# Two-way decay scans of an AdaLN-attention-MoE layer: decays read from PSUM, no scaling of the forward scan, a later numerator bonus, and an earlier x added by GpSimd

## The chip, the cores and the metric

The kernel is one program on one core of a Trainium2 chip. The metric is the device time of one launch in microseconds (us), as the median of several executions. TensorE (PE), VectorE (DVE), ScalarE (ACT), GpSimd (POOL) and the DMA queue that SyncE (SP) issues to run side by side and meet at semaphores.

## The reference

For each of 4 sequences (512 tokens, 512 channels) the layer runs a two-way decaying scan, an RWKV-like mixing block, a second scan, and a routed feed-forward part (32 experts, 8 per token). The part that the change touches, cut short:

```python
def _bi_wkv(r, k, v, w, u, time_emb):
    tf = sigmoid(sum(time_emb))
    decay = exp(-exp(w)) * (0.5 + 0.5 * tf)          # one number per channel and sequence
    ek = exp(min(k, 30)); ekv = ek * v
    nf, df = forward  scans a = a*decay + ekv,  b = b*decay + ek
    nb, db = backward scans of the same
    euk = exp(min(u + k, 30))
    num = nf + nb - ekv + euk * v
    den = df + db - ek + euk
    return sigmoid(r) * num / max(den, 1e-8) * (0.8 + 0.2 * tf)

x1 = bi_wkv(x, side, side, w, u, cond)
h = layernorm(x1); xr, xk, xv = mu*h + (1-mu)*shift(h)
x1 = x1 + (sigmoid(xr Wr) * ek*v/(ek+1e-8)) Wout
h2 = layernorm(x1)                                   # two mixes of it
x = x + x1 + sigmoid(xr2 cWr) * (relu(xk2 cWk)**2 cWv)
x = x + ffn(bi_wkv(x, side, side, w2, u2, cond))
```

## The kernel before

Everything is kept as 128 channels by 512 tokens in fp32, so that one tile is a quarter (K = 4) of a sequence (B = 4). One scan tile is an *item*: a sequence b, a quarter k and a scan w (0 is the first, 1 the second). 32 items pass through a pipeline of *slots*, one item each, spread over three engines:

- DVE, `slot`: `fwd` runs two forward scans (numerator L1312, denominator L1313) into `F` and makes the start values of the backward scans (`ini`, L1315); `clip` caps the keys of the next item (L1302, L1303); one instruction multiplies both forward scans by (1 - decay) times (1 + decay) (L1348), which makes one backward scan of the result equal to forward plus backward minus the doubled term; `fin` of the item before (L1340); `bwd` runs the two backward scans (L1324), adds the bonus `EU` to the denominator (L1328) and floors it (L1330, which signals `den_ready`).
- ACT: `pre` takes the exponentials of the next item's keys (L1079, L1080), `post` makes the inverse of the denominator as exp(-ln) (L1086, L1088).
- POOL: `mid` makes ekv and euk*v of the next item (L1008, L1009), `post` adds the bonus to the numerator (L1015) as soon as the backward scans are done, then multiplies numerator and denominator by the inverse (L1017, L1019). `fin` waits for these.

The decay is a 128x1 column of an SBUF table, read by the scans as a broadcast row.

Around the slots a software pipeline runs over the sequences: a prologue (4 items of sequence 0, layer norm and mixes of it), 4 items of sequence 1 with the first projections, then a loop of two iterations of 8 slots each, and a last iteration of 8 slots. Iteration b does, beside its slots, the gates and projections of sequence b, layer norm 2 and the second mixing of sequence b-1, and layer norm 1 of sequence b+1. `center`, `normalise` and `mixes` are DVE's part of a layer norm, `own` (L1128) is ACT's part of the mixing, `product`, `residual`, `final_a` and `y_stage` are DVE steps that read or feed the matmuls. At an iteration's end `add_mix` on POOL adds the mixing result to x (L1047), `x_new` adds that to the residual stream (L1416), and `x_side` (L1423) forms the tile that is stored.

All order is the order in which each engine's program is written; engines wait on counting semaphores. A layer norm's mean goes to PSUM bank 5, its variance to bank 6. After the loops come the routing, a scatter by POOL, the expert matmuls and the output.

## Time and profile before

| | us |
|---|---|
| median of 3 runs | 1420.02 (1419.4 to 1423.0) |
| the profiled execution | 1419.25 |
| its span in the profile | 1417.5 |
| PE / DVE / ACT / POOL busy in the span | 1124.3 / 835.8 / 452.9 / 707.3 |
| granted TensorE clock, mean | 0.921 |

The span divides into a part with scans (up to about 680 us) and a part without. Busy sums over the whole span mix the two, so the reading goes by stretches.

### The profile page before, as it was taken

Reading aid. Unit: us, or ns where it says so; the run is one execution under the profiler, and the core shown is the slowest. Engines: PE = TensorE matmul, PEld = TensorE weight load, DVE = VectorE, ACT = ScalarE, POOL = GpSimd, SP = SyncE. Lnnn points to the kernel's source line nnn. Section 1 sums busy time; section 2 is a strip of 40 time slices with the busy share of each in tenths; the row PEclk is TensorE's granted clock in tenths of the full one; section 3 lists DMA queues with packets and bytes.
Section 4 is the critical chain, followed back from the end, with each engine's and each line's share of the span. In section 5 each row is a group of like instructions: output and inputs, shape, how many; then the busy total and the mean of one; then the engine's idle time right before and its main releaser. Section 6 shows DMA issues by size and latency. Waiting matters only on the chain.

```text
span 1417.5 us, 14264 instructions
## 1 busy us (share of the span) xinstructions
PE 1124.3 (79%) x3686; PEld 653.7 (46%) x3687; DVE 835.8 (59%) x1409; ACT 452.9 (32%) x692; POOL 707.3 (50%) x493
## 2 busy tenths in 40 slices
PE   0155698558963789637899999999799999999938
PEld 0022243223421334213545444444688888888823
DVE  8777568979788995997607830000344444444424
ACT  2233345243352334431412120210233334333310
POOL 5616305645237442566010276775277777777730
PEclk9978799879987789869999999999899999999969
DMA  4979401001110111021412077226677777777685
GB/s 130 363 261 351 144 0 37 15 31 66 59 37 15 37 60 59 30 89 55 177 59 89 37 243 251 106 108 204 158 127 130 128 126 124 126 129 129 96 203 183
DMA packets 132114, 169.11 MB, mean 119 GB/s; under 512 B 9456, under 2 KB 104688, under 8 KB 132080
## 3 DMA queue, kind: packets, MB, share of 16 engines
q1 hardware_dynamic: 102896, 129.37, 29.5%
q0 software_dynamic: 29184, 39.34, 15.0%
q8 instruction: 15, 0.25, 0.1%
q14 instruction: 19, 0.16, 0.0%
HBM read 84.92 MB, written 83.76 MB: 119 GB/s over the span
## 4 chain that ended last, share of the span: by engine, by line
PE 36%; DVE 20%; POOL 18%; issue 18%; DMA 5%; ACT 3%; SPq 0%; POOLq 0%; DVEq 0%; ACTq 0%
PE banks L520 10%; PE banks L541 10%; POOL slots_in L407 9%; DVE arena L1324 4%; PE banks L1530 4%; PE banks L457 4%; PE banks L510 3%; PE banks L531 2%; POOL arena L1009 2%; DVE arena L1401 2%; POOL arena L1008 2%; DVE arena L1328 2%; POOL arena L1019 2%; DMA slots_in<-arena 2%; POOL arena L1015 2%
## 5 line engine op out<-in xcount | busy, mean ns | idle before, releaser
L1530 PE MATMUL banks<-arena 128*128 128x512 f32 x896 | 420.6, 630 | 162.0 <-ACT arena L1145 67.7
L1530 PEld LDWEIGHTS banks<-arena 128*128 128x128 f32 x896 | 179.8, 203 | 400.9 <-issue 237.3
L420 POOL DMA_INDIRECT sums<-arena x160 | 249.5, 1559 | 119.6 <-ACT arena L646 86.7
L457 PE MATMUL banks<-arena 128*128 128x512 f32 x576 | 252.5, 599 | 10.0 <-ACT arena L620 7.1
L407 POOL DMA_INDIRECT slots_in<-arena x128 | 130.1, 1017 | 103.0 <-issue 43.8
L457 PEld LDWEIGHTS banks<-arena 128*128 128x128 f32 x576 | 109.9, 192 | 149.7 <-issue 135.2
L1008 POOL TENSOR_TENSOR arena<-arena 128x512 f32<-128x512 f32 x32 | 64.2, 2006 | 210.4 <-ACT arena L1080 210.4
L520 PE MATMUL banks<-arena 128*128 x640 | 153.3, 383 | 0.0
L541 PE MATMUL banks<-arena 128*128 x640 | 151.2, 379 | 0.0
L807 DVE SCALAR_TENSOR_TENSOR arena<-arena 128x256 f32<-128x256 f32 x160 | 72.1, 490 | 89.5 <-ACT arena L631 89.5
L520 PEld LDWEIGHTS banks<-arena 128*128 128x128 f32 x640 | 116.5, 192 | 13.3 <-issue 0.4
L541 PEld LDWEIGHTS banks<-arena 128*128 128x128 f32 x640 | 115.4, 190 | 12.4
L790 DVE COPY arena<-banks 128x512 f32<-128x512 f32 x80 | 55.3, 691 | 90.8 <-PE banks L510 90.8
L858 DVE TENSOR_TENSOR arena<-arena,banks 128x512 f32<-128x512 f32 x16 | 11.0, 686 | 159.5 <-PE banks L457 159.5
L1324 DVE TENSOR_TENSOR_SCAN arena<-arena 128x512 f32<-128x512 f32 x64 | 104.4, 1671 | 0.2
L631 ACT ACTIVATE arena<-banks 128x512 f32<-128x512 f32 x80 | 47.8, 597 | 162.8 <-PE banks L520 162.8
L1548 PE MATMUL banks<-arena 128*128 128x512 f32 (+1 forms) x64 | 33.8, 670 | 69.7 <-DVE arena L1367 69.6
L1086 ACT ACTIVATE arena<-arena 128x512 f32<-128x512 f32 x32 | 20.1, 630 | 190.4 <-DVE arena L1330 190.4
L646 ACT ACTIVATE arena<-banks 128x512 f32<-128x512 f32 x80 | 47.8, 597 | 90.7 <-PE banks L541 90.7
L1017 POOL TENSOR_TENSOR arena<-arena 128x512 f32<-128x512 f32 x32 | 51.0, 1595 | 47.8 <-ACT arena L1088 47.8
L1401 DVE SCALAR_TENSOR_TENSOR arena<-arena 128x511 f32<-128x511 f32 x80 | 73.7, 974 | 2.0 <-ACT arena L1128 2.0
L617 ACT ACTIVATE arena<-banks 128x512 f32<-128x512 f32 x32 | 19.1, 597 | 164.3 <-PE banks L457 164.3
(169 smaller groups left out, 1418.2 us busy)
## 6 DMA issues: line engine op xcount, KB each, us to landing
slots_in<-arena SPq DMA_DIRECT2D x8, 2800.0 KB, 17.1
arena<-slots_in SPq DMA_DIRECT2D x80, 280.0 KB, 3.2
sums<-arena SPq DMA_DIRECT2D x4, 2176.0 KB, 20.3
arena<-fT SPq DMA_DIRECT2D x32, 256.0 KB, 2.7
arena<-w2T SPq DMA_DIRECT2D x4, 2048.0 KB, 21.4
arena<-w1T SPq DMA_DIRECT2D x4, 2048.0 KB, 12.1
arena<-sums SPq DMA_DIRECT2D x16, 512.0 KB, 8.8
arena<-xT SPq DMA_DIRECT2D x5, 1024.0 KB, 5.6
```

Of the source, the lines that this page charges most:

```text
L407: pool.indirect_dma_start(rows_in, bass.IndirectOffsetOnAxis(ap=POSU[:, n, j:j + 1], axis=0), XLR[:, n], None).then_inc(S['scattered'], 16)
L420: pool.indirect_dma_start(sums[g % RING], bass.IndirectOffsetOnAxis(ap=DESTU[:, g:g + 1], axis=0), YO[:, i % 4, c], None, compute_op=ALU.add)\
L457: ins = pe.matmul(out, w[:, k, m * P:(m + 1) * P], x[k], start=(k == 0), stop=(k == kt - 1))
L520: ins = pe.matmul(bank(2 + q % 2)[:, c * INTER:(c + 1) * INTER], XTB[:, q % 2, c, k], W1[:, bass.ds(e[c], 1), k].rearrange("p o i -> p (o ...
L541: ins = pe.matmul(bank(6 + q % 2)[:, c * LAT:(c + 1) * LAT], HTB[:, q % 2, c, k], W2[:, bass.ds(e[c], 1), k].rearrange("p o i -> p (o i)") ...
L790: dve.tensor_copy(XTB[:, q % 2].rearrange("p c k s -> p (c k s)"), bank(q % 2)).then_inc(S['xT_copied'], 1)
L807: ins = dve.scalar_tensor_tensor(HB[:, q % 2, c], HB[:, q % 2, c], WS[:, bass.ds(2 * i + c, 1)], HB[:, q % 2, c], ALU.mult, ALU.mult)
L1008: pool.tensor_tensor(EV, EK, KV[:, par], ALU.mult).then_inc(S['ev_ready'], 1)
L1017: pool.tensor_tensor(F[:, par, 1], F[:, par, 1], INV, ALU.mult)
L1324: ins = dve.tensor_tensor_scan(F[:, par, n, ::-1], d, F[:, par, n, ::-1], ini[:, par, n:n + 1], ALU.mult, ALU.add)
L1401: ins = dve.scalar_tensor_tensor(out[:, k, 1:T], H[:, k, 1:T], column(RESTG, name, k), out[:, k, 1:T], ALU.mult, ALU.add)
L1530: ins = pe.matmul(out, w[:, k, m * P:(m + 1) * P], x[:, k], start=(k == 0), stop=(k == kt - 1))
```

## The change

What it does:

- The decay table is copied once to PSUM bank 6 (`DECAY`), and all four scans of an item read their decay column from there. Mean and variance of a layer norm now share bank 5 (`STAT`).
- The multiplication by (1 - decay)(1 + decay) (`rest`) is gone from `slot`. The scans stay unscaled; the ratio num/den needs the factor only against the bonus, so the factor is folded into ACT's columns (`less_log`, `log_rest`, `rest`), into the floor (`floors`) and into the start values (`over_rest`). These columns are made once, in the prologue, by a short chain between DVE and ACT.
- POOL's numerator bonus waits for `den_ready` instead of `bwd_done`.
- `add_mix` is replaced by `add_x`: POOL adds x to the residual stream of sequence b-1 at the start of slots 3 to 6 of iteration b, and DVE's `x_new` adds the mixing result directly. The load of x is issued at the head of the iteration instead of near its end.
- `normalise` has one small instruction fewer, and its large one is split in two halves; ACT's `own` starts after the first half.

```diff
+        DECAY = psum[:, 6, 0:2 * K * B].rearrange("p (w k b) -> p w k b", w=2, k=K)
+        STAT = psum[:, 5, :]
@@ SP, iteration
+                    if prev and n == 0:
+                        load_x_again(b - 1)
...
                 elif prev:
-                    load_x_again(b - 1)
                     load_final(b - 1, 0)
@@ POOL
             def post(it):
-                pool.wait_ge(S['bwd_done'], i + 1)
+                pool.wait_ge(S['den_ready'], i + 1)
...
+                    if adds and 3 <= n < 3 + K:
+                        add_x(b - 1, n - 3)
...
-            def add_mix(b):
-                pool.wait_ge(S['xf_loaded'], 16 * (b + 1))
-                for m in range(K):
-                    pool.wait_ge(S['v2_evac'], 4 * b + m + 1)
-                    pool.tensor_tensor(XF[:, m], XF[:, m], R2S[:, m], ALU.add).then_inc(S['x_summed'], 1)
+            def add_x(b, m):
+                if m == 0:
+                    pool.wait_ge(S['z2_ready'], b + 1)
+                    pool.wait_ge(S['xf_loaded'], 16 * (b + 1))
+                whole = XN[:, bass.ds(b, 1), m].rearrange("p o t -> p (o t)")
+                pool.tensor_tensor(whole, whole, XF[:, m], ALU.add).then_inc(S['x_summed'], 1)
@@ ACT
-                act.activation(EU[:, par], EU[:, par], ACT.Exp).then_inc(S['keys_exp'], 1)
+                act.activation(EU[:, par], EU[:, par], ACT.Exp, bias=dcol_of(less_log, it)).then_inc(S['keys_exp'], 1)
...
-                step.did(act.activation(INV, F[:, par, 1], ACT.Ln))
+                step.did(act.activation(INV, F[:, par, 1], ACT.Ln, scale=dcol_of(rest, it)))
                 step.wait()
-                act.activation(INV, INV, ACT.Exp, scale=-1.0).then_inc(S['inv_ready'], 1)
+                act.activation(INV, INV, ACT.Exp, scale=-1.0, bias=dcol_of(log_rest, it)).then_inc(S['inv_ready'], 1)
@@ DVE
-                d = dcol(it).to_broadcast([P, T])
+                d = dcol_of(DECAY, it).to_broadcast([P, T])
                 dve.tensor_tensor_scan(F[:, par, 0], d, EV, 0.0, ALU.mult, ALU.add)
...
-                dve.tensor_scalar(F[:, par, 1], F[:, par, 1], DEN_FLOOR, None, ALU.max).then_inc(S['den_ready'], 1)
+                dve.tensor_scalar(F[:, par, 1], F[:, par, 1], dcol_of(floors, it), None, ALU.max)\
+                   .then_inc(S['den_ready'], 1)
...
-                step.did(dve.tensor_scalar(F[:, it['par']], F[:, it['par']], rest[:, it['w'], it['k'], bass.ds(it['b'], 1)],
-                                           None, ALU.mult))
...
-                step.did(dve.tensor_scalar(TMP, TMP, -0.5, 1.5, ALU.mult, ALU.add))
+                step.did(dve.scalar_tensor_tensor(RS, TMP, 3.0, RS, ALU.subtract, ALU.mult))
                 step.wait()
-                step.did(dve.tensor_tensor(RS, RS, TMP, ALU.mult))
-                step.wait()
-                rs = RS.rearrange("p (o t) -> p o t", o=1).to_broadcast([P, K, T])
-                dve.tensor_tensor(H[:, :, 1:T + 1], H[:, :, 1:T + 1], rs, ALU.mult)\
-                   .then_inc(S[f'norm{which}_ready'], 1)
+                half = K // 2
+                rs = RS.rearrange("p (o t) -> p o t", o=1).to_broadcast([P, half, T])
+                for k in range(0, K, half):
+                    dve.tensor_tensor(H[:, k:k + half, 1:T + 1], H[:, k:k + half, 1:T + 1], rs, ALU.mult)\
+                       .then_inc(S[f'norm{which}_ready'], 1)
...
                 dve.wait_ge(S['x_summed'], 4 * b + m + 1)
-                dve.tensor_tensor(xn(b, m), xn(b, m), XF[:, m], ALU.add).then_inc(S['xnew_ready'], 1)
+                dve.wait_ge(S['v2_evac'], 4 * b + m + 1)
+                dve.tensor_tensor(xn(b, m), xn(b, m), R2S[:, m], ALU.add).then_inc(S['xnew_ready'], 1)
```

How this moves instructions, first on DVE, for one slot of the first four items (`arena` is all of SBUF, `banks` is PSUM; a scan is listed as SCALAR_TENSOR_TENSOR). Before:

```order
L1312 SCALAR_TENSOR_TENSOR arena<-arena 128x512
L1313 SCALAR_TENSOR_TENSOR arena<-arena 128x512
L1315 TENSOR_SCALAR arena<-arena 128x2
L1302 TENSOR_SCALAR arena<-arena 128x512
L1303 TENSOR_SCALAR arena<-arena 128x512
L1348 TENSOR_SCALAR arena<-arena 128x1024
L1340 SCALAR_TENSOR_TENSOR arena<-arena 128x512
L1324 SCALAR_TENSOR_TENSOR arena<-arena 128x512 x2
L1328 TENSOR_TENSOR arena<-arena 128x512
L1330 TENSOR_SCALAR arena<-arena 128x512
```

The same slot on DVE in the changed kernel:

```order
L1339 SCALAR_TENSOR_TENSOR arena<-banks,arena 128x512
L1340 SCALAR_TENSOR_TENSOR arena<-banks,arena 128x512
L1342 TENSOR_SCALAR arena<-arena 128x2
L1329 TENSOR_SCALAR arena<-arena 128x512
L1330 TENSOR_SCALAR arena<-arena 128x512
L1367 SCALAR_TENSOR_TENSOR arena<-arena 128x512
L1350 SCALAR_TENSOR_TENSOR arena<-banks,arena 128x512 x2
L1354 TENSOR_TENSOR arena<-arena 128x512
L1356 TENSOR_SCALAR arena<-arena 128x512
```

The four scans have a PSUM input where they had an SBUF one, the 128x1024 multiplication is gone, and nothing else changes place.

On POOL, the end of a loop iteration before: the last slot's five products and sums, then the four additions of `add_mix`:

```order
L1008 TENSOR_TENSOR arena<-arena 128x512
L1009 TENSOR_TENSOR arena<-arena 128x512
L1015 TENSOR_TENSOR arena<-arena 128x512
L1017 TENSOR_TENSOR arena<-arena 128x512
L1019 TENSOR_TENSOR arena<-arena 128x512
L1044 REGISTER_ALU
L1046 ISA
L1047 TENSOR_TENSOR arena<-arena 128x512
L1046 REGISTER_ALU
L1047 TENSOR_TENSOR arena<-arena 128x512
```

In the changed kernel the additions stand between `post` of one slot (L1023, L1025, L1027) and `mid` of the next (L1016, L1017), here at the start of slot 3:

```order
L1023 TENSOR_TENSOR arena<-arena 128x512
L1025 TENSOR_TENSOR arena<-arena 128x512
L1027 TENSOR_TENSOR arena<-arena 128x512
L1056 REGISTER_ALU
L1058 ISA
L1058 TENSOR_TENSOR arena<-arena 128x512
L1013 REGISTER_ALU
L1016 TENSOR_TENSOR arena<-arena 128x512
L1017 TENSOR_TENSOR arena<-arena 128x512
```

One addition each went from behind the last slot to the head of slots 3, 4, 5 and 6.

On SP's queue the load of x (L906, 128x4x512) now stands at the loop's head between two loads of keys (L889):

```order
L889 ISA [waits euv_ready]
L889 DMA arena<-fT 128x512
L906 ISA
L906 DMA arena<-xT 128x4x512
L887 REGISTER_ALU
L889 ISA [waits euv_ready]
L889 DMA arena<-fT 128x512
```

It stood behind the last store of `q_scratch`, ahead of the two loads of `q_scratch`.

## Rows read from the trace of the kernel before

**Rows 1.** Stretches: length, then busy us (count) of PE, PEld, DVE, ACT, POOL; clock, DMA.

```profile
373.90:543.30 169.40, 121.18 (x256) 52.02 (x255) 144.01 (x151) 65.41 (x92) 81.91 (x48) 0.84 0.13 43
543.30:680.10 136.80, 95.73 (x209) 41.32 (x209) 120.30 (x121) 48.60 (x68) 76.25 (x45) 0.85 0.19 62
```

**Rows 2.** Timeline of DVE over one full slot: start, duration, instruction.

```profile
262.30 1.21 DVE L1312 TENSOR_TENSOR_SCAN arena<-arena 128x512 f32<-128x512 f32 x1
...
264.66 1.05 DVE L1315 TENSOR_SCALAR arena<-arena 128x2 f32<-128x2 f32 x1
...
265.96 1.49 DVE L1303 TENSOR_SCALAR arena<-arena 128x512 f32<-128x512 f32 x1
267.37 0.74 DVE L1348 TENSOR_SCALAR arena<-arena 128x1024 f32<-128x1024 f32 x1
268.03 0.68 DVE L1340 SCALAR_TENSOR_TENSOR arena<-arena 128x512 f32 x1
268.63 3.41 DVE L1324 TENSOR_TENSOR_SCAN arena<-arena 128x512 f32<-128x512 f32 x2
272.08 1.57 DVE L1328 TENSOR_TENSOR arena<-arena 128x512 f32<-128x512 f32 x1
273.68 1.37 DVE L1330 TENSOR_SCALAR arena<-arena 128x512 f32<-128x512 f32 x1
274.97 1.21 DVE L1312 TENSOR_TENSOR_SCAN arena<-arena 128x512 f32<-128x512 f32 x1
```

**Rows 3.** Timeline of POOL over the same slot.

```profile
263.78 1.91 POOL L1017 TENSOR_TENSOR arena<-arena 128x512 f32<-128x512 f32 x1 [1.69 <-ACT arena L1088]
265.65 1.52 POOL L1019 TENSOR_TENSOR arena<-arena 128x512 f32<-128x512 f32 x1
268.71 2.25 POOL L1008 TENSOR_TENSOR arena<-arena 128x512 f32<-128x512 f32 x1 [1.54 <-ACT arena L1080]
270.93 2.17 POOL L1009 TENSOR_TENSOR arena<-arena 128x512 f32<-128x512 f32 x1
273.06 1.71 POOL L1015 TENSOR_TENSOR arena<-arena 128x512 f32<-128x512 f32 x1
```

**Rows 4.** DVE and POOL at the start of a `normalise`, from both timelines.

```profile
338.45 0.75 DVE L1383 SCALAR_TENSOR_TENSOR arena<-banks,arena 128x512 f32<-128x512 f32 x1 [2.60 <-ACT arena L1118]
339.24 1.06 DVE L1385 TENSOR_TENSOR arena<-arena 128x512 f32<-128x512 f32 x1
...
338.49 1.27 POOL L1019 TENSOR_TENSOR arena<-arena 128x512 f32<-128x512 f32 x1
```

**Rows 5.** Stretches of single slots and of the mixes, columns as in rows 1.

```profile
398.85:408.97 10.12, 0.26 (x1) 0.00 (x0) 10.02 (x13) 6.79 (x10) 3.13 (x3) 0.77 0.30 104
420.66:431.50 10.84, 10.84 (x27) 4.84 (x26) 10.74 (x12) 1.15 (x2) 6.06 (x3) 1.00 0.04 5
467.37:477.79 10.42, 6.12 (x15) 2.42 (x13) 10.28 (x12) 3.73 (x5) 5.58 (x3) 0.91 0.00 0
479.98:492.28 12.30, 10.98 (x20) 4.83 (x21) 12.20 (x12) 4.19 (x5) 8.78 (x5) 0.75 0.14 43
515.92:530.06 14.14, 14.14 (x29) 6.06 (x28) 14.14 (x20) 5.70 (x9) 6.19 (x4) 0.84 0.29 107
589.42:625.60 36.18, 17.33 (x41) 7.41 (x39) 35.87 (x34) 5.97 (x10) 24.93 (x13) 0.77 0.23 78
625.60:661.52 35.92, 29.98 (x64) 12.77 (x64) 35.56 (x32) 14.78 (x22) 22.78 (x13) 0.90 0.11 39
```

**Rows 6.** Timeline of DVE: four mixes without and with POOL beside them.

```profile
515.92 2.72 DVE L1401 SCALAR_TENSOR_TENSOR arena<-arena 128x511 f32<-128x511 f32 x4
519.23 4.75 DVE L1401 SCALAR_TENSOR_TENSOR arena<-arena 128x511 f32<-128x511 f32 x4
```

**Rows 7.** Timeline of ACT: an activation with a column operand, and one without.

```profile
392.56 0.69 ACT L1116 ACTIVATE arena<-banks,arena 128x512 f32<-128x512 f32 x1
393.27 0.63 ACT L1118 ACTIVATE arena<-arena 128x512 f32<-128x512 f32 x1
```

More of the change, by code:

```diff
@@ L111, in build @@
         vec = place(len(VECTORS), K)
-        small = place(64)
+        small = place(40)
         tf = small[:, 0:4]
@@ L120, in build @@
         condT = small[:, 32:36]
-        decay = place(2, K, B)
         rest = place(2, K, B)
-        scratch32 = place(2, K, B)
+        over_rest, floors, log_rest, less_log = (place(2, K, B) for _ in range(4))
         ini = place(2, 2)
         MIXES = ['mu_r', 'mu_k', 'mu_v', 'cm_mu_r', 'cm_mu_k']
-        MUG, RESTG, FIRSTB = (place(len(MIXES), K) for _ in range(3))
+        mix_columns = place(3, len(MIXES), K)
+        MUG, RESTG, FIRSTB = (mix_columns[:, n] for n in range(3))
         XN = place(B, K, T)
@@ L143, in build @@
         RS, TMP = (place(T) for _ in range(2))
+        decay, scratch32 = (TMP[:, n * 32:n * 32 + 2 * K * B].rearrange("p (w k b) -> p w k b", w=2, k=K) for n in range(2))
         def q2_again(b, m):
@@ L1055, in _ @@
             with pool.Fori(1, B - 1) as b:
-                slots(body_items(b), body_items(b + 1)[0], b, USUAL)
-                add_mix(b - 1)
-            slots(last_items, None, B - 1, USUAL)
-            add_mix(B - 2)
-            add_mix(B - 1)
+                slots(body_items(b), body_items(b + 1)[0], b, USUAL, True)
+            slots(last_items, None, B - 1, USUAL, True)
+            for m in range(K):
+                add_x(B - 1, m)
             part3_pool(pool)
@@ L1115, in rsqrt @@
                     act.wait_ge(S['xs_ready'], 4 * b)
[L1116 removed]
+                step.did(act.activation(RS, STAT, ACT.Ln, bias=eps_col))
                 step.wait()
@@ L1122, in own @@
             def own(which, b):
-                act.wait_ge(S[f'norm{which}_ready'], b + 1)
                 for n, (name, out) in enumerate(zip(*mixed(which))):
@@ L1127, in own @@
                     for k in range(K):
+                        if n == 0 and k % 2 == 0:
+                            act.wait_ge(S[f'norm{which}_ready'], 2 * b + k // 2 + 1)
                         act.activation(out[:, k], H[:, k, 1:T + 1], ACT.Identity, scale=column(MUG, name, k),
@@ L1210, in _ @@
             ln_exp()
+            act.wait_ge(S['rest_ready'], 1)
+            step.did(act.activation(log_rest, rest, ACT.Ln))
+            step.wait()
+            act.activation(less_log, log_rest, ACT.Exp, scale=-1.0).then_inc(S['log_exp'], 1)
+            act.wait_ge(S['columns_ready'], 1)
             pre(first_items[0])
@@ L1285, in _ @@
             step.did(dve.tensor_tensor(rest, rest, scratch32, ALU.mult))
+            dve.tensor_copy(DECAY, decay)
             step.wait()
-            def dcol(it):
-                return decay[:, it['w'], it['k'], bass.ds(it['b'], 1)]
+            dve.tensor_scalar(rest, rest, 1e-12, None, ALU.max).then_inc(S['rest_ready'], 1)
+            dve.wait_ge(S['rest_ready'], 1)
+            step.did(dve.reciprocal(scratch32, rest))
+            step.wait()
+            step.did(dve.tensor_tensor(over_rest, decay, scratch32, ALU.mult))
+            step.did(dve.tensor_scalar(floors, scratch32, DEN_FLOOR, None, ALU.mult))
+            dve.wait_ge(S['log_exp'], 1)
+            step.wait()
+            step.did(dve.tensor_tensor(scratch32, less_log, rest, ALU.mult))
+            step.wait()
+            step.did(dve.scalar_tensor_tensor(log_rest, scratch32, -1.0, log_rest, ALU.add, ALU.add))
+            step.wait()
+            dve.tensor_scalar(less_log, log_rest, -1.0, None, ALU.mult).then_inc(S['columns_ready'], 1)
             def xn(b, m):
@@ L1507, in _ @@
             residual(0, 3)
-            base, one = step.n, 8 * 3 + 2 * 4
+            base, one = step.n, 8 * 2 + 2 * 3
             with dve.Fori(1, B - 1) as b:
@@ L1547, in mean @@
                         pe.wait_ge(S['y_tile' if which == 1 else 'o_evac'], 4 * b + k + 1)
-                    ins = pe.matmul(bank(5), ones, src[:, k], start=(k == 0), stop=(k == K - 1))
+                    ins = pe.matmul(STAT, ones, src[:, k], start=(k == 0), stop=(k == K - 1))
                 ins.then_inc(S[f'mean{which}_done'], 1)
@@ L1554, in var @@
                 for k in range(K):
-                    ins = pe.matmul(bank(6), ones, src[:, k], start=(k == 0), stop=(k == K - 1))
+                    ins = pe.matmul(STAT, ones, src[:, k], start=(k == 0), stop=(k == K - 1))
                 ins.then_inc(S[f'var{which}_done'], 1)
```

22 lines of the change are left out of this document (11 added, 11 removed).

## The prediction, made before the changed kernel ran

> **What bounds the kernel now.** I read the busy times by stretch first. In a loop iteration of 169.4 us DVE is busy for 144.0 and PE for 121.2; in the last iteration DVE for 120.3 of 136.8, PE for 95.7 [rows 1]. So DVE sets the pace where there are scans, PE has some 48 us of idle time per iteration, and whatever shortens DVE's chain ahead of about 680 us moves all that follows.
>
> Then the timelines of DVE and POOL over one slot, which give what DVE is busy *with*. A slot lasts 12.67 us (262.30 to 274.97). A forward scan alone takes 1.21 us, but the two backward scans take 3.41 where 2 x 1.13 is expected; the addition takes 1.57 and the floor 1.37, the 128x2 product 1.05 [rows 2]. POOL in the same time needs 2.25, 2.17 and 1.71 for products that take 1.27 when it is alone [rows 3, 4]. Set side by side they take turns: POOL's first product is issued at 268.71 while the first backward scan runs (to about 269.77), then runs to 270.93; the second scan runs to about 272.07, and then POOL's second product, to 273.10; DVE's addition ends 0.55 later; POOL's addition follows, to 274.77; DVE's floor ends 0.28 after that. Each of these instructions excludes the other engine's. Some 4.5 of the 12.67 us are DVE waiting inside its own instructions.
>
> **What frees them.** Whether a PSUM operand takes an instruction out of this exclusion is shown at the start of a `normalise`: L1383, with its first input in PSUM and its second in SBUF, runs 338.45 to 339.20 in 0.75 us, and POOL's product beside it takes 1.27, undelayed. The next DVE instruction, with both inputs in SBUF, takes 1.06: it ends 0.55 after POOL's product [rows 4]. The changed scans have just that operand form. The Trainium skill says the same (SBUF — State Buffer, "Who interferes with whom": a Vector instruction with at most one SBUF input, outside the two-port modes, doesn't contend with GpSimd). The trace agrees.
>
> **A slot after the change.** I redo the turn-taking from the durations above, with 0 at the first forward scan.
>
> - *Full slot* (POOL still busy with the item before). POOL's bonus addition runs 0.1 to 1.4 beside the scans, which is free: ACT's ln and exp fill the same 1.5 us. The two products by the inverse run from 1.6 to 2.9 and, with the caps between them, to 4.35 (as 263.78 to 267.17 now). ACT's instructions with a column operand cost 0.06 more each (0.69 against 0.63) [rows 7]; that is in these numbers, twice in the inverse and once in the keys. DVE's scans end at 2.3, the start value waits to 2.9, the caps end at 4.55, the scaling (0.66) is gone, `fin` runs to 5.1. The backward scans, free now, end at 7.4. POOL's products for the next item run from 5.9 (1.26 after the caps, as now, and 0.06) to 8.4. DVE's addition waits for the second, ends at 8.95, and the floor, no longer behind POOL's addition, at 9.4. The next slot starts at 9.3: 3.35 less than 12.67.
> - *With `add_x` in it* (slots 3 and 4): the addition goes in front of `fin` and holds it for 1.2, but DVE loses most of that where it waited for POOL anyway: 9.5, so 3.15 less. `fin` behind slot 4 has no such cover: add_x is issued right as the last product ends and holds it 1.1; with the column operands 1.25 dearer.
> - *POOL idle at its start* (slot 2, 10.84 [rows 5]): 8.0, 2.85 less. Without `fin` (slot 5, 10.42; slot 0 is alike): 7.9, 2.5 less. Slot 6 (12.30), whose forward scans are held now too: 8.65, 3.65 less, `add_x` included. Slot 1 (10.12) is held by ACT's eight `own` in front of the exponentials; these start 1.1 earlier with the split `normalise`: 1.05 less.
>
> **A loop iteration.** Slots 0 to 7: 2.5 + 1.05 + 2.85 + 3.15 + 3.15 + 2.5 + 3.65 + 3.35 = 22.2. The mixes of layer norm 1 lose POOL's `add_mix`: four of them take 4.75 with it beside them and 2.72 without [rows 6], the stretch of 14.14 comes to about 10.6 [rows 5]: 3.5. The two normalises: one small instruction less (0.4 each, like a cap or a floor let in at once), 0.2 each for the split and for ACT's columns: 0.4. Against that the mixes of layer norm 2 get POOL's later addition beside them: -0.6, and `fin` behind slot 4: -1.25. Sum 24.3 of 169.4, twice: 48.6. The row of loads and stores at the iteration's end keeps its length. PE's work of 121 fits into 145; following its order, the mean that opens the next iteration is ready some 2.5 us before DVE wants it.
>
> **The rest.** Last iteration: slots 2 to 4 take 36.18 now and 8.0 + 9.5 + 9.5 = 27.0 after, slots 5 to 7 take 35.92 and 29.5 (ACT is late there with two matmul results, so slot 6 has to wait for its ekv), slot 0 gives 2.5 [rows 5]; less 0.9, since PE's row of 48 matmuls is then the last to finish: 17.4 with the normalise. Prologue: the four first slots give 3.5 + 3 x 3.35 and the layer norm 1.3, the new columns cost 2.2, an estimate (nine tiny instructions in a chain at 0.25; a floor of 512 elements takes 0.28 once it is let in): 12.7. (The very first slot gives 3.5 rather than 2.5, as its first forward scan is held by POOL now.) Second group of four: 2.5 + 2.85 + 3.35 + 2.85, less 0.4 for handoffs, and 0.6 of its layer norm, since PE sets the end there: 11.7. Tail, behind 680 us: 1.2. The load of x moves to a place where 16 DMA engines are 13% busy [rows 1], ahead of a key load that isn't wanted for 20 us: nothing; if it delayed that load, the caps of slot 1 would wait up to 3.
>
> **The unknown price** is that of a scan that reads PSUM. No row has one. Below: nothing, as the scan's own rate (1.13 for 512 elements, against 0.6 for `fin`) is what it waits for. Above: L1383's 0.75 against `fin`'s 0.68 [rows 2, 4], 0.07 for each of 128 scans, 9 us. I take 1.6 in all, near the lower end, as half of the scans lie under POOL's products. The Trainium skill gives VectorE a fixed 120 cycles for a PSUM source and 58 for SBUF (VectorE: DVE Perf Modes, "The TRN2 errata"). By that 65 ns a scan, an estimate, the gain would be 8 us less. The row beside it shows 0.07 at most, so it can't be excluded.
>
> Sum: 48.6 + 17.4 + 12.7 + 11.7 + 1.2 - 1.6 = 90. The profiled execution took 1419.25, so 1329; it lies 0.8 under the median of 1420.02.
>
> **Rivals.**
> 1. *PE takes over* (0.14). DVE's chain gets shorter and PE, at a clock of 0.84 in that stretch, doesn't come along: its 121 us of 145 are no slack if the matmuls between the second squaring and the next mean, about 50 us of them in a row, run behind DVE by 5 to 10 more. That takes 7 from each of three iterations: 1350. For it: a margin of only 2.5 us. Against: the low clock comes after its idle waits, and these shrink.
> 2. *The scans still exclude POOL* (0.05), the change doesn't do what it says. Then only the scaling goes (32 x 0.66 = 21), the mixes give 7, the norms 4, the 12 `add_x` cost 1.2 each and the prologue 2: 1403. Rows 4 speak against it.
> 3. *A scan with a PSUM operand is slow* (0.03), the other side. 128 scans; it decides from 90/128 = 0.7 us each, a scan of 1.9 instead of 1.2. If the read added another 512 steps like those of the present one (1.07 each), 137 us come on top: 1466. Against it: L1383 pays at most 0.07.
> 4. *More than forecast* (0.08): PE's clock rises with denser work, or the caps find POOL idle more often. 1312.
>
> The forecast itself has 0.70 (1318 to 1344). The range must hold 8 in 10: 1316 to 1353, which takes in the dearer scan (1337) and rival 1. A difference of 0.3% (4 us) is about what this measurement can tell. Faster by more than that 0.96 (forecast, rivals 1, 2, 4 nearly whole), within 0.01, slower 0.03.
>
> **What the profile after would show.** Scans of 1.2 us everywhere, the backward pair 2.4 at all times, even where POOL is busy; full slots of 9.3 and 9.5; POOL's first product of a slot 1.3 instead of 2.25; DVE's addition still 1.0 to 1.6, held by POOL; iterations of 145; mixes of layer norm 1 of 2.7 for each four; the stretch behind the scans as long as before. Wrong would be: a pair of 3.4 (rival 2), a lone scan above 1.3 (rival 3), DVE idle before its `center` with PE as releaser (rival 1), or a stage behind the scans that changes its length.

## The result, and the profile of the changed kernel

The changed kernel takes **1343.39 us** (median of 4 runs, 1342.74 to 1344.24), the kernel before 1419.71 beside it (4 runs). The ratio is 0.9455, 95% interval 0.9443 to 0.9467; measured once more it was 0.9454 (0.9440 to 0.9469). The profiled execution has a span of 1341.7 us where that of before had 1417.5: 75.8 less. I had forecast 90 less, 1329 us, with 1316 to 1353 as the range. The profiles of two experiments below, fills_behind_x and scaling_kept, are of slow executions (1401.2 and 1409.1 us, where their fastest took 1377.3 and 1388.2); only their part ahead of the last `x_new` is used, in which slots that the edits don't touch last as long as in the changed kernel.

The two stretches of [rows 1], in the changed kernel (columns as there):

```profile
339.26:487.57 148.31, 117.35 (x258) 50.45 (x257) 119.85 (x143) 67.64 (x92) 64.07 (x48) 0.91 0.15 50
487.57:605.89 118.32, 96.55 (x213) 41.44 (x212) 100.50 (x114) 50.89 (x68) 60.80 (x45) 0.91 0.24 78
```

DVE is busy for 24.2 us less in a loop iteration, the iteration is 21.1 shorter, and TensorE's mean granted clock is 0.91 of 2.4 GHz instead of 0.84. PE is busy for 117.4 of 148.3. The page's groups of the backward scans and of POOL's first product (busy us, mean ns; the second one's mean was 2006), and the `center` that opens this iteration:

```profile
L1350 DVE TENSOR_TENSOR_SCAN arena<-banks,arena 128x512 f32<-128x512 f32 x64 | 78.3, 1264 | 0.0
L1016 POOL TENSOR_TENSOR arena<-arena 128x512 f32<-128x512 f32 x32 | 42.0, 1314 | 195.7 <-ACT arena L1090 195.7
```

```profile
339.26 2.29 DVE L1403 TENSOR_TENSOR arena<-arena,banks 128x2048 f32<-128x2048 f32 x1
```

The full slot, which [rows 2, 3] show before. Its undisturbed form after the change stands in the prologue; first DVE, then POOL, from the timelines:

```profile
29.25 1.22 DVE L1339 TENSOR_TENSOR_SCAN arena<-banks,arena 128x512 f32<-128x512 f32 x1
30.38 1.20 DVE L1340 TENSOR_TENSOR_SCAN arena<-banks,arena 128x512 f32<-128x512 f32 x1
31.61 0.59 DVE L1342 TENSOR_SCALAR arena<-arena 128x2 f32<-128x2 f32 x1
32.12 0.41 DVE L1329 TENSOR_SCALAR arena<-arena 128x512 f32<-128x512 f32 x1
32.45 1.48 DVE L1330 TENSOR_SCALAR arena<-arena 128x512 f32<-128x512 f32 x1
33.85 0.68 DVE L1367 SCALAR_TENSOR_TENSOR arena<-arena 128x512 f32<-128x512 f32 x1
34.46 2.44 DVE L1350 TENSOR_TENSOR_SCAN arena<-banks,arena 128x512 f32<-128x512 f32 x2
36.94 1.38 DVE L1354 TENSOR_TENSOR arena<-arena 128x512 f32<-128x512 f32 x1
38.35 0.49 DVE L1356 TENSOR_SCALAR arena<-arena 128x512 f32<-128x512 f32 x1
38.75 1.22 DVE L1339 TENSOR_TENSOR_SCAN arena<-banks,arena 128x512 f32<-128x512 f32 x1
```

```profile
35.28 1.26 POOL L1016 TENSOR_TENSOR arena<-arena 128x512 f32<-128x512 f32 x1 [1.63 <-ACT arena L1090]
36.51 1.26 POOL L1017 TENSOR_TENSOR arena<-arena 128x512 f32<-128x512 f32 x1
38.91 1.27 POOL L1023 TENSOR_TENSOR arena<-arena 128x512 f32<-128x512 f32 x1 [1.15 <-DVE arena L1356]
```

The backward pair takes 2.44 although POOL's first product (35.28 to 36.54) runs wholly beside it, and that product takes 1.26 where it took 2.25. What is left of the turn-taking is L1354: both its inputs are in SBUF, and it ends 0.55 behind POOL's second product. The floor behind it takes 0.49, as POOL's addition now starts 0.07 after it. The slot lasts 9.50 us instead of 12.67.

Inside the loop the same slot, with `add_x` in it, looks like this (DVE, then POOL):

```profile
392.32 1.20 DVE L1340 TENSOR_TENSOR_SCAN arena<-banks,arena 128x512 f32<-128x512 f32 x1
393.68 0.68 DVE L1342 TENSOR_SCALAR arena<-arena 128x2 f32<-128x2 f32 x1 [0.15 <-DVE arena L1340]
...
396.03 1.74 DVE L1367 SCALAR_TENSOR_TENSOR arena<-arena 128x512 f32 x1
397.69 2.44 DVE L1350 TENSOR_TENSOR_SCAN arena<-banks,arena 128x512 f32<-128x512 f32 x2
400.17 0.69 DVE L1354 TENSOR_TENSOR arena<-arena 128x512 f32<-128x512 f32 x1
401.02 0.48 DVE L1356 TENSOR_SCALAR arena<-arena 128x512 f32<-128x512 f32 x1 [0.15 <-DVE arena L1354]
401.42 1.22 DVE L1339 TENSOR_TENSOR_SCAN arena<-banks,arena 128x512 f32<-128x512 f32 x1
```

```profile
393.06 1.26 POOL L1025 TENSOR_TENSOR arena<-arena 128x512 f32<-128x512 f32 x1 [0.44 <-ACT arena L1098]
...
395.77 1.45 POOL L1058 TENSOR_TENSOR arena<-arena 128x512 f32 x1
397.44 1.46 POOL L1016 TENSOR_TENSOR arena<-arena 128x512 f32<-128x512 f32 x1 [0.22 <-ACT arena L1090]
```

It lasts 10.23. `add_x` (L1058) holds `fin` for 1.06 (1.74 for 0.68), of which the shorter L1354 gives 0.69 back. And ahead of L1342 and of L1356 stand 0.15 us each that neither the prologue nor [rows 2] have. Ahead of L1356 they are paid in full. L1342 is held by POOL in any case: it ends 0.04 behind POOL's product by the inverse (L1025), and that one now starts 0.20 later in the slot than in the prologue, as POOL waits 0.44 for ScalarE's inverse instead of 0.24.

**Where the 75.8 us came from.** Times between DVE's first scans and its `center` instructions, from the timelines of both kernels; the forecast is that of my terms.

| stretch | before | after | gain | forecast |
|---|---|---|---|---|
| up to the first forward scan | 10.4 | 11.9 | -1.6 | -2.2 |
| first group of four, to its `center` | 60.9 | 47.6 | 13.3 | 13.6 |
| layer norm of batch 0 | 25.5 | 24.0 | 1.5 | 1.3 |
| second group, to its `center` | 70.5 | 70.1 | **0.5** | **11.1** |
| layer norm 1 of batch 1 | 38.2 | 38.4 | -0.2 | 0.6 |
| loop iteration, twice | 168.4, 169.4 | 147.3, 148.3 | **21.0, 21.1** | **24.3 each** |
| last iteration | 136.9 | 118.3 | 18.6 | 17.4 |
| everything behind | 737.4 | 735.8 | 1.6 | 1.2 |
| price of a scan from PSUM | | | in the rows above | -1.6 |

The repeated kernel, changed_again, shows how far these rows can be trusted: its full slots are the same within 0.01, but its layer norm of batch 1 takes 37.2 instead of 38.4 and its iterations 147.9 and 149.5. So a single row of the table is good to about 1 us.

Two places miss. The first is in the second group. DVE, ScalarE and the queue of SyncE there, from three timelines of the changed kernel:

```profile
138.07 0.68 DVE L1383 TENSOR_TENSOR arena<-arena,banks 128x512 f32<-128x512 f32 x1
149.16 1.41 DVE L1392 SCALAR_TENSOR_TENSOR arena<-arena 128x512 f32<-128x512 f32 x2 [10.42 <-ACT arena L1151]
...
148.50 1.29 ACT L1151 ACTIVATE arena<-arena 128x512 f32<-128x512 f32 x2 [12.62 <-DMA arena<-xT]
...
116.21 8.45 SPq L941 DMA_DIRECT2D slots_in<-arena  x2
124.70 8.51 SPq L946 DMA_DIRECT2D sums<-arena  x1
136.57 6.00 SPq L902 DMA_DIRECT2D arena<-xT  x2
```

DVE scales x tiles by their sigmoids in `y_stage`; for tiles 2 and 3 it waits 10.4 us. ScalarE has been waiting 12.6 for their load, which SyncE issued at 136.57, behind the last group of zero fills of `slots_in` and `sums`. In the kernel before the same lines read:

```profile
126.55 7.87 SPq L934 DMA_DIRECT2D slots_in<-arena  x2
134.46 7.62 SPq L939 DMA_DIRECT2D sums<-arena  x1
160.41 2.02 SPq L895 DMA_DIRECT2D arena<-xT  x2
```

The page's row of DMA throughput in 40 slices of 33.5 us shows the fills in its first five:

```profile
GB/s 164 359 328 333 166 0 39 16 47 47 89 36 23 47 94 25 70 101 145 63 95 31 219 292 110 103 207 167 122 128 122 127 131 128 121 128 131 86 224 179
```

In the kernel before the fills had been issued by 142 and had 18 us to drain before the load of x was wanted. The last group takes about as long to issue as before (8.4 and 8.5 us, against 7.9 and 7.6), DVE comes 24 us earlier, and the load now stands in line: ScalarE can start 11.9 us after its issue. The Trainium skill (DMA: Bandwidth & Descriptors, "Queues, rings and completion order") says that each DMA engine takes the descriptors of one ring in their order. The traces agree: the same two issues take 2.0 us behind a drained queue and 6.0 behind a full one, and with the fills behind the load instead of ahead of it (fills_behind_x, below) ScalarE starts 2.5 us after the issue.

### The profile page after: what moved, and what is told of

Read it like the earlier page. It is cut to its first block, busy times and chain, and to the rows that moved or that the text cites. A ratio compares the mean times of both kernels' runs of the same rounds, so it can differ in the third digit from the quotient of the medians.

```text
span 1341.7 us, 14332 instructions
## 1 busy us (share of the span) xinstructions
PE 1114.9 (83%) x3686; PEld 649.9 (48%) x3687; DVE 742.0 (55%) x1385; ACT 462.4 (34%) x694; POOL 636.6 (47%) x493
## 3 DMA queue, kind: packets, MB, share of 16 engines
q0 software_dynamic: 29184, 39.34, 15.9%
## 4 chain that ended last, share of the span: by engine, by line
PE 39%; DVE 28%; POOL 12%; issue 9%; DMA 7%; ACT 4%; DVEq 1%; SPq 0%; POOLq 0%; ACTq 0%
PE banks L527 10%; PE banks L548 10%; POOL slots_in L414 9%; DVE arena L1350 6%; PE banks L1556 5%; PE banks L464 4%; DVE arena L1426 4%; PE banks L517 3%; PE banks L538 3%; DVE arena L1354 2%; DVE arena L1340 2%; DVE arena L1367 2%; DVE arena L1339 2%; DMA slots_in<-arena 2%; DVE arena L1330 2%
## 5 line engine op out<-in xcount | busy, mean ns | idle before, releaser
L1556 PE MATMUL banks<-arena 128*128 128x512 f32 x896 | 412.6, 620 | 97.9 <-ACT arena L1156 44.6
L464 PE MATMUL banks<-arena 128*128 128x512 f32 x576 | 251.3, 597 | 10.0 <-ACT arena L627 7.1
L1016 POOL TENSOR_TENSOR arena<-arena 128x512 f32<-128x512 f32 x32 | 42.0, 1314 | 195.7 <-ACT arena L1090 195.7
L1350 DVE TENSOR_TENSOR_SCAN arena<-banks,arena 128x512 f32<-128x512 f32 x64 | 78.3, 1264 | 0.0
L1034 POOL TENSOR_TENSOR arena<-arena 128x512 f32<-128x512 f32 x16 | 23.3, 1459 | 101.5 <-ACT arena L1111 101.5
L1426 DVE SCALAR_TENSOR_TENSOR arena<-arena 128x511 f32<-128x511 f32 x80 | 68.8, 917 | 0.0
L1139 ACT ACTIVATE arena<-arena 128x512 f32<-128x512 f32 x80 | 57.3, 801 | 28.3 <-DVE arena L1417 28.3
```

The source lines that it names most:

```text
L464: ins = pe.matmul(out, w[:, k, m * P:(m + 1) * P], x[k], start=(k == 0), stop=(k == kt - 1))
L1139: act.activation(out[:, k], H[:, k, 1:T + 1], ACT.Identity, scale=column(MUG, name, k), bias=V(f'ln{which}_b', k)).then_inc(S[f'own{which} ...
L1350: ins = dve.tensor_tensor_scan(F[:, par, n, ::-1], d, F[:, par, n, ::-1], ini[:, par, n:n + 1], ALU.mult, ALU.add)
L1426: ins = dve.scalar_tensor_tensor(out[:, k, 1:T], H[:, k, 1:T], column(RESTG, name, k), out[:, k, 1:T], ALU.mult, ALU.add)
L1556: ins = pe.matmul(out, w[:, k, m * P:(m + 1) * P], x[:, k], start=(k == 0), stop=(k == kt - 1))
```

## The experiments

The twelve runs fall into three sets, each with the kernel before measured in it: the first four of the table, the next four, and the last four. In the first two sets the kernel before took 63 and 48 us longer than in the third (1483.6 and 1469.0, against 1420.6). The traces show the excess of the tried kernels behind the last `x_new`: that part takes 689 to 735 us there, and 669 to 670 in the third set and in the changed kernel. What makes it longer is not shown, and the changed kernel itself was not run in those two sets. Times of whole kernels can't be compared across sets, so I compare the **start of the last `x_new`** (four in one row of DVE's timeline, L1442 in the changed kernel): 746.1 us before, 672.3 in the changed kernel, 673.1 in the repeated one, which shows how far it repeats. The ratio to the kernel before is given where it was measured.

| run | last `x_new` | against 672.3 | ratio to before |
|---|---|---|---|
| fills_behind_x | 664.5 | -7.8 | 0.9341 (0.9294 to 0.9389) |
| adds_in_gap | 668.6 | -3.7 | 0.9434 (0.9395 to 0.9473) |
| one_column | 666.6 | -5.7 | 0.9476 (0.9445 to 0.9507) |
| decay_in_sbuf | 725.2 | +52.9 | 0.9843 (0.9810 to 0.9875) |
| psum_alone | 688.2 | +15.9 | none on record; 1377.8 to 1410.0 us, before 1469.0 |
| scaling_kept | 687.3 | +15.0 | 0.9541 (0.9496 to 0.9585) |
| numerator_early | 686.4 | +14.1 | 0.9584 (0.9561 to 0.9607) |
| add_at_end | 672.7 | +0.4 | 0.9499 (0.9462 to 0.9535) |
| changed_again | 673.1 | +0.8 | 0.9454 (0.9440 to 0.9469) |
| fills_and_gap | 658.9 | -13.4 | 0.9357 (0.9344 to 0.9371) |
| static_columns | 668.2 | -4.1 | 0.9412 (0.9399 to 0.9425) |
| all_three | 654.1 | -18.2 | 0.9327 (0.9314 to 0.9340) |

### What the decays in PSUM are worth

**decay_in_sbuf** takes that one thing away. The table lies in eight rows of `vec` that are dead by then.

```diff
-        DECAY = psum[:, 6, 0:2 * K * B].rearrange("p (w k b) -> p w k b", w=2, k=K)
+        DECAY = None
+        DEAD = MIXES + ['cond_w', 'cond2_w', 'ln1_g']
...
-            dve.tensor_copy(DECAY, decay)
+            for n, name in enumerate(DEAD):
+                dve.tensor_copy(vec[:, VECTORS.index(name)], decay[:, n // K, n % K])
```

> The changed kernel, with the table of decays that the scans read in SBUF instead of PSUM, nothing else changed. Theory: the scans and POOL's products exclude each other again; backward pairs take 3.4 instead of 2.45 and POOL's first product of a slot 2.25 instead of 1.26; of the gain only the missing scaling and the smaller parts are left: 1398 us (1385 to 1408). Rival: the gain comes from the missing scaling and from the order of the slot, and the operand's place adds little: 1350 to 1360, with backward pairs that stay near 2.5.

Measured: 52.9 us later at the last `x_new`; the full slot lasts 12.14. DVE, then POOL, from its timelines:

```profile
35.43 2.22 DVE L1345 TENSOR_TENSOR_SCAN arena<-arena 128x512 f32<-128x512 f32 x1
...
40.99 3.41 DVE L1355 TENSOR_TENSOR_SCAN arena<-arena 128x512 f32<-128x512 f32 x2
...
36.54 2.18 POOL L1029 TENSOR_TENSOR arena<-arena 128x512 f32<-128x512 f32 x1
...
43.28 2.17 POOL L1021 TENSOR_TENSOR arena<-arena 128x512 f32<-128x512 f32 x1
```

The same scan takes 1.20 with its decay in PSUM and 2.22 with it in SBUF when POOL is busy. On 1343.4 that makes 1396, where the theory had 1398; the rival (1350 to 1360) is refuted. The Trainium skill's rule (SBUF — State Buffer, "Who interferes with whom": a Vector instruction with two SBUF inputs contends with a GpSimd instruction that reads SBUF, one with a single SBUF input doesn't) is thereby shown for scans, both ways.

**psum_alone** is the converse: the kernel before, with the decays in PSUM and, to make room for them, both layer norm sums in bank 5. Nothing else is changed.

```diff
-                d = dcol(it).to_broadcast([P, T])
+                d = dcol(it, DECAY).to_broadcast([P, T])
...
-                    ins = pe.matmul(bank(6), ones, src[:, k], start=(k == 0), stop=(k == K - 1))
+                    ins = pe.matmul(bank(5), ones, src[:, k], start=(k == 0), stop=(k == K - 1))
```

> The kernel before, with one part of the change alone: the scans read their decays from PSUM (and both layer norm sums share one bank). Scaling, numerator, additions of x as before. Theory: the operand's place is most of the gain: a slot's scans lose 1.0 in the backward pair and POOL's products 0.9 each, about 1.7 of each of 32 slots: 1365 us (1355 to 1378). Rival: with the scaling and the early numerator in place POOL and DVE still exclude each other in as much of the slot, and little comes: 1400 or more.

Measured: the last `x_new` at 688.2, 57.9 before that of the kernel before; the full slot lasts 10.17 instead of 12.67. So the operand's place gives 57.9 of the 73.8 us that lie ahead of `x_new`. From this start the other parts together give 15.9, and 1.1 more at the end of the last `x_new`, whose four additions take 3.57 us here and 2.49 in the changed kernel.

### What the other parts are worth

**scaling_kept** puts an instruction of the scaling's size back.

```diff
                 dve.wait_ge(S['fwd_done'], it['i'] + 1)
+                step.did(dve.tensor_scalar(F[:, it['par']], F[:, it['par']], 1.0, None, ALU.mult))
                 if it['prev'] is not None:
                     fin(it['prev'])
+                step.wait()
                 bwd(it)
```

> The changed kernel, with a multiplication of the 128x1024 sums by 1.0 between the forward scans and fin, where the scaling by the rest column was. Theory: it takes 0.66 plus a handoff in each of 32 slots and stands on DVE's chain, save where fin waits for POOL anyway (22 us of such waits in all): 1343 + 32 x 0.6 = 1362 (1355 to 1368). Rival: it lies under the waits for POOL nearly everywhere: 1350 or less.

Measured: +15.0, inside the range, but not by the mechanism that I gave. The full slot of the prologue is **9.52** with the scaling and 9.50 without. Its DVE rows:

```profile
43.64 0.68 DVE L1375 TENSOR_SCALAR arena<-arena 128x1024 f32<-128x1024 f32 x1
44.24 0.68 DVE L1367 SCALAR_TENSOR_TENSOR arena<-arena 128x512 f32<-128x512 f32 x1
44.85 2.44 DVE L1350 TENSOR_TENSOR_SCAN arena<-banks,arena 128x512 f32<-128x512 f32 x2
47.33 0.79 DVE L1354 TENSOR_TENSOR arena<-arena 128x512 f32<-128x512 f32 x1
```

L1354 takes 0.79 instead of 1.38: whatever comes ahead of it is paid out of its wait for POOL's second product. Most of the price is paid where `add_x` is in the slot, 11.92 us against 10.23, since POOL then holds two instructions of DVE instead of one (slots 0 and 5 of an iteration pay another 0.5 each):

```profile
400.13 1.76 DVE L1375 TENSOR_SCALAR arena<-arena 128x1024 f32<-128x1024 f32 x1
401.82 1.75 DVE L1367 SCALAR_TENSOR_TENSOR arena<-arena 128x512 f32 x1
```

**numerator_early** lets POOL's bonus addition wait for the backward scans again.

```diff
-                pool.wait_ge(S['den_ready'], i + 1)
+                pool.wait_ge(S['bwd_done'], i + 1)
                 pool.wait_ge(S['euv_ready'], i + 1)
```

> The changed kernel, with POOL's bonus addition waiting for the backward scans again instead of for the denominator. Theory: it then holds DVE's floor by up to 1.2 (the floor takes 1.4 instead of 0.49), and ends no later than what needs it; with some 0.8 in each of 32 slots: 1366 (1358 to 1372). Rival: DVE's two instructions and POOL's take turns in either order, and the inverse, not the numerator, is what fin waits for: within 4 us of 1343.

Measured: +14.1, between theory and rival. In the full slot it costs what was expected, 10.40 instead of 9.50; DVE's floor is held to the end of POOL's addition (DVE's two rows, then POOL's):

```profile
37.79 1.38 DVE L1354 TENSOR_TENSOR arena<-arena 128x512 f32<-128x512 f32 x1
39.21 1.37 DVE L1356 TENSOR_SCALAR arena<-arena 128x512 f32<-128x512 f32 x1
...
38.58 1.71 POOL L1023 TENSOR_TENSOR arena<-arena 128x512 f32<-128x512 f32 x1
```

Slots 0, 1 and 5 take no longer with it (slot 5 8.00 for 7.99), so that five of eight pay, 0.8 each. And the wait for x in the second group takes up part of what the prologue loses (`center` of batch 0 comes 3.6 later, that of batch 1 only 1.2).

**add_at_end** moves the additions of x back to the iteration's end, and the load of x with them.

```diff
-                slots(body_items(b), body_items(b + 1)[0], b, USUAL, True)
+                slots(body_items(b), body_items(b + 1)[0], b, USUAL)
+                add_mix(b - 1)
...
-                dve.tensor_tensor(xn(b, m), xn(b, m), R2S[:, m], ALU.add).then_inc(S['xnew_ready'], 1)
+                dve.tensor_tensor(xn(b, m), xn(b, m), XF[:, m], ALU.add).then_inc(S['xnew_ready'], 1)
```

> The changed kernel, with the additions of x back at the iteration's end as before (POOL adds x to the value tiles beside the mixes of layer norm 1). Theory: the early additions cost the slots about what they give the mixes: slots 3, 4, 6 and the lone fin get 3 us shorter, the mixes 3.5 longer, so the whole stays within 4 us of 1343 (1341 to 1348). Rival, by the terms of my forecast: the slots hide them (0.2 each) and only the mixes lose, some 1.5 to 2.5 per iteration, and more in the tail: 1349 or more.

Measured: +0.4, as the theory has it. In an iteration the end behind slot 6 takes 48.3 instead of 44.8 (the 3.5 of my forecast), and the slots give back 2.4: slot 3 9.85 for 10.23, slot 4 with its `fin` 20.84 for 22.11, slot 6 8.38 for 9.10. The start of the last `x_new` doesn't move by more than a repetition does (0.8). Its four additions take 3.57 us instead of 2.49, though, as they wait for POOL's again, so that they end 1.5 later. That is all that this part can be credited with.

### Where the missing 14 us went

**fills_behind_x** issues the last group of fills behind the loads of x.

```diff
-                    if not prev:
+                    if not prev and n < K - 1:
                         zero_slots(2 * n)
...
                     load_x(b + 1, 3)
+                    zero_slots(2 * K - 2)
+                    zero_slots(2 * K - 1)
+                    zero_sums(K - 1)
```

> The changed kernel, with the last of the four groups of zero fills (two parts of slots_in and one of sums) issued behind the loads of x tiles 2 and 3 instead of ahead of them. Theory: the step that failed is the transfers of the prologue; VectorE waits 10.4 us at 138.75 us for the sigmoid of an x tile whose load stands behind 17 us of fills. With the fills behind it the load takes about 2 us again, the wait falls to some 2 to 3 us, and all that follows moves up by 7 to 9: 1335.5 us (1333 to 1338). Rival: the fills hold the stretch by their sum, and leave it as long wherever they stand (the wait moves to the squaring of layer norm 2 in the next iteration, which waits for the last fill): 1343.

Measured: -7.8; `center` of batch 1 at 143.98 instead of 153.55. DVE, then the queue:

```profile
138.20 0.67 DVE L1386 TENSOR_TENSOR arena<-arena,banks 128x512 f32<-128x512 f32 x1
139.83 0.75 DVE L1395 SCALAR_TENSOR_TENSOR arena<-arena 128x512 f32<-128x512 f32 x1 [0.96 <-ACT arena L1154]
142.01 0.75 DVE L1395 SCALAR_TENSOR_TENSOR arena<-arena 128x512 f32<-128x512 f32 x1 [1.43 <-ACT arena L1154]
...
136.70 2.00 SPq L902 DMA_DIRECT2D arena<-xT  x2
138.75 5.18 SPq L941 DMA_DIRECT2D slots_in<-arena  x2
143.97 8.82 SPq L946 DMA_DIRECT2D sums<-arena  x1
```

The wait of 10.4 falls to 0.96 and 1.43. The squaring in the next iteration, which needs the last fill, still waits for DVE's `center` (8.64 us, as in the changed kernel) and not for the fill. The rival is refuted.

**one_column** reads the small columns at a fixed batch.

```diff
+        def same_column(table, it):
+            return table[:, it['w'], it['k'], 1:2]
...
-                act.activation(EU[:, par], EU[:, par], ACT.Exp, bias=dcol_of(less_log, it)).then_inc(S['keys_exp'], 1)
+                act.activation(EU[:, par], EU[:, par], ACT.Exp, bias=same_column(less_log, it)).then_inc(S['keys_exp'], 1)
```

> The changed kernel, with the five small columns (decay over rest, floors, rest, its log, less_log) read at batch 1 always instead of at the running batch, so that their addresses need no register; the decays of the scans stay as they are. Left out: the right column for the other batches. Theory: the 0.15 us ahead of the 128x2 product and ahead of the floor, which only the slots of the loop show, and 0.27 more in ScalarE's inverse there, come from addresses that are computed behind a wait; without them 16 loop slots get 0.3 to 0.45 shorter: 5 to 7 us, 1337.5 (1335 to 1340). Rival: the time is only shown in another place, or lies under POOL's work: 1343.

Measured: -5.7. The 0.15 us are gone from all slots, and POOL waits 0.23 for the inverse instead of 0.44; slot 3 takes 9.91 instead of 10.23, slot 2 8.15 for 8.38, slot 6 8.79 for 9.10, an iteration 145.4 and 146.3 for 147.3 and 148.3. DVE, then POOL, in slot 3:

```profile
389.70 0.60 DVE L1345 TENSOR_SCALAR arena<-arena 128x2 f32<-128x2 f32 x1
...
389.00 1.27 POOL L1028 TENSOR_TENSOR arena<-arena 128x512 f32<-128x512 f32 x1 [0.23 <-ACT arena L1101]
```

**adds_in_gap** moves the four additions of x to where POOL is idle for 11.8 us.

```diff
-                    if adds and 3 <= n < 3 + K:
-                        add_x(b - 1, n - 3)
                     for m in gates.get(n, ()):
                         gate_product(b, m)
+                    if adds and n == 1:
+                        for m in range(K):
+                            if m == 2:
+                                pool.wait_ge(S['norm2_ready'], 2 * b)
+                            add_x(b - 1, m)
```

> The changed kernel, with the four additions of x to the residual moved from the slots 3 to 6 into slot 1, behind the second gate product: two at once, two when the normalise of layer norm 2 is done. POOL is idle there for 11.8 us (355.9 to 367.7), DVE waits 6.3 us for ScalarE and then runs forward scans. Theory: in slots 3, 4 and 6 and at the fin behind slot 4 each addition holds DVE's fin by 1.06 (1.74 instead of 0.68), which costs some 0.6 a slot and 1.25 at the lone fin: 3 us in each of two iterations, 1 in the last, so 1336.5 (1335 to 1339). Rival: slots are held by POOL's chain anyway and the additions cost in the gap what they cost before: 1343.

Measured: -3.7, half of what I expected. The slots give what was expected (3: 9.84 for 10.23; 4 with its `fin`: 20.81 for 22.11; 6: 8.37 for 9.10), 2.4 per iteration, and the two iterations get 2.3 and 1.9 shorter, where I had put 3. The last one gets 0.8 shorter (117.6 for 118.3): its last scans start 1.4 earlier, and what follows takes 26.1 instead of 25.5. The slots behave as the theory has it; the size of the whole was too large, and the other half went in stretches that repeat only to about 1 us, so where is not shown.

### A version that is faster than both

**changed_again** is the changed kernel, unaltered, as the measure of the third set.

> The changed kernel once more, unaltered, as the measure for the others of this call: their tails, behind 672 us, may be longer or shorter on this chip than in the first runs. Expected: x_new ends at 672.3 us within 1 us, as in the first profile, whatever the tail takes; ratio to the kernel before 0.945 to 0.953.

Measured: 1343.27 us (5 runs), last `x_new` at 673.1.

**fills_and_gap** has the edits of fills_behind_x and adds_in_gap.

> The changed kernel with two edits: the last group of fills behind the loads of x (alone it moved the last x_new from 672.3 to 664.5 us) and the four additions of x in slot 1 (alone 668.6). Theory: the two act in different stretches and add up: x_new at 660.8 us (659.5 to 662), 11.5 us less than the changed kernel in the whole. Rival: the mixes and waits of later iterations give part of it back to PE: 663 or more.

Measured: 1330.54 us (1328.39 to 1331.35), `x_new` at 658.9: they add up (11.5), and give 1.9 more than that, just below the range that I gave. The gain in the whole is 12.7 us against 11.5 expected.

**static_columns** has POOL copy each iteration's columns to fixed places.

```diff
+            pool.wait_ge(S['columns_ready'], 1)
             with pool.Fori(1, B - 1) as b:
+                for table, *ats in PLACES.values():
+                    for w in range(2):
+                        ins = pool.tensor_copy(vec[:, ats[w]],
+                                               table[:, w, :, bass.ds(b - 1 if w else b + 1, 1)].rearrange("p k o -> p (k o)"))
+                ins.then_inc(S['columns_now'], 1)
```

> The changed kernel, in whose loop POOL copies the ten rows of small columns that belong to the iteration to fixed places at its top, where it is idle for 12 us; VectorE and ScalarE read the fixed places. The result is that of the changed kernel. Theory: it gives what reading one fixed column gave (x_new at 666.6 instead of 672.3), less little, as the copies lie in idle time: 667 (666 to 669). Rival: the copies, ten instructions with addresses from a register, take over 1 us each on POOL or hold VectorE, and the gain is gone: 671 or more.

Measured: 1338.01 us (1336.03 to 1339.12), `x_new` at 668.2, with slots 2, 3, 5 and 6 of 8.14, 9.90, 7.86 and 8.78 as in one_column. This edit gives the right result for every sequence, which one_column doesn't.

**all_three** has all three edits.

> The three edits together: fills behind the loads of x, the additions of x in slot 1, and fixed places for the columns. Theory: 7.8 + 3.7 + 5 less: x_new at 656 us (654.5 to 658), and 16 us less than the changed kernel in the whole, about what my forecast had been (1329 against 1343). Rival: POOL's copies and the additions meet, or the wait for ScalarE grows by what the slots lose: 660 or more.

Measured: **1325.50 us** (1324.35 to 1327.16), ratio 0.9327 (0.9314 to 0.9340): 17.8 less than the changed kernel and 95 less than the kernel before. Its last `x_new`, at 654.1, is 0.4 ahead of the range. Its iterations take 142.8 and 144.3 us, slot 3 lasts 9.53. An iteration's row, as in [rows 1]:

```profile
325.36:469.68 144.32, 116.98 (x258) 50.47 (x257) 117.87 (x143) 67.64 (x92) 63.56 (x48) 0.92 0.16 51
```

## Why the prediction came out as it did

The time lay in the range, and the mechanism was the one that I had named, but the figure is 14 us above mine and only 0.6 below the edge of the likeliest case (1344). That the range held it is partly luck: I had widened it upwards for a dear scan and for PE taking over, neither of which occurred, and most of the 14 us came from two things that the prediction doesn't mention, a transfer and the addresses of the new columns.

- **The scans leave the exclusion: right.** Pairs take 2.44 to 2.45, POOL's first product 1.31 on average over 32 instead of 2.01. psum_alone and decay_in_sbuf put the part at 53 to 58 us. Rival 2 (1403) is refuted by them.
- **The full slot of 9.3: 9.50.** The steps ended at 2.95 (start value, forecast 2.9), 4.7 (caps, 4.55), 5.3 (`fin`, 5.1), 7.65 (backward scans, 7.4), 8.5 (POOL's products, 8.4), 9.1 (addition, 8.95). The backward pair is 2.45, not the 2.3 that I took.
- **The price of a scan from PSUM: nothing.** 1.22 and 1.20 us, before 1.21 or 1.22 and 1.19 or 1.20 where POOL was idle, at most 0.01. I took 1.6 us in all. The 120 cycles against 58 which the Trainium skill gives (VectorE: DVE Perf Modes, "The TRN2 errata") don't show in a scan with one input in PSUM and one in SBUF. Rival 3 is out.
- **`add_x` in a slot at 0.2: 0.4.** One_column has such slots at 9.91 and the prologue has 9.50 without it. Slot 6 pays 0.7 (9.10 for 8.38) and lasts 9.10 instead of 8.65. The `fin` behind slot 4, priced at 1.25, costs 0.9: 1.27 for both, less the 0.38 of slot 4.
- **What I left out: addresses from a register.** "ACT's instructions with a column operand cost 0.06 more" was in the sum, the column's address was not. In the kernel before, the start value used the same column as the scans ahead of it and shows no such time; the two new columns of DVE stand behind a wait, and each shows 0.15 us there. With ScalarE's three it is about 2 us per iteration (one_column; static_columns agrees within the repetition). The operands themselves cost 0.09 each on ScalarE, 0.72 against the 0.63 of the kernel before, and not the 0.06 of [rows 7]. That it is the register instruction that takes this time is shown only in so far as a fixed column takes it away. The other 1.2 of the 3.2 that an iteration misses should be the 0.2 of each full slot and the longer operands; no run takes these apart, and 1.2 is what a repetition can move an iteration by.
- **The step that failed: the second group's 11.7, with "the load of x moves to a place where 16 DMA engines are 13% busy: nothing".** That sentence dealt with the load that the change moves, in the loop. It didn't ask which transfer becomes late when DVE reaches the second group 24 us earlier. [Rows 1] begin at 374 us, and my sum has no row of SyncE's queue ahead of 170, where 31 MB of fills (8 of 2.8 MB, 4 of 2.2 MB) go out at 330 to 360 GB/s. The stretch gained 0.5 instead of 11.1. fills_behind_x gives 9.6 of it back at `center`, of which 7.8 reach the last `x_new`.
- **Small terms.** The columns cost 1.6 at the first scan (forecast 2.2). The mixes of layer norm 1 take 2.72 for each four, as forecast. The last iteration gave 18.6 (17.4), the tail 1.6 (1.2).
- **PE takes over (rival 1, 1350): no.** DVE has no idle time ahead of its `center` in either loop iteration: the mean is there when DVE, which waits for the loads of `q_scratch` just before, gets to it. The clock rose from 0.84 to 0.91. The waits in the two normalises grew by 0.4 each (6.30 for 5.91, 2.98 for 2.60), but not for PE: with fixed columns they are 6.10 and 2.78, so half comes from the addresses, and the rest matches the 0.18 by which ScalarE's two instructions of the inverse are longer.
- **The parts don't add up one by one.** Each taken away from the whole, they are worth 53, 15, 14 and 0: 82 where the whole is 74. The changes in `normalise` were not tried by themselves. The scaling, which I priced at 0.66 a slot, costs nothing in a full slot, as the wait for POOL's second product absorbs it, and 1.7 in a slot with `add_x`.

## What to carry to other kernels

When two engines wait for each other inside their instructions, the durations of one form, with the other engine idle and busy, show it (1.2 against 2.2 here), and one operand in PSUM can end it. An edit that makes an engine reach a stage 24 us earlier has to be followed into every queue that feeds this stage, down to transfers that the edit doesn't touch. When an addition on one engine holds the instructions of another (`fin` 1.74 us instead of 0.68), it belongs where the other waits or runs forms that it doesn't hold, and an operand whose address comes from a register is best not placed right behind a wait.
